# Attention tower: the PSUM banks of the scores apart from those of all other work, v times W0 per tile, and the rounding of q and k on GpSimd

## What is computed

```
h = conv1d(sign(x), sign(kernel), 3 taps), bias and batch norm      # 4 x 748 x 64
z = layernorm(h)
qkv = z @ Wqkv + bqkv; q, k, v = reshape(qkv, (3, b, n, d, h))     # 8 heads of 64
score = einsum('bnqh,btqh->bnth', q, k) * d ** -0.5
attn = softmax(score, axis=1)
av = einsum('bnnh,bnqh->bnqh', attn, v)       # only the DIAGONAL of attn is used
h = h + av.reshape(b, n, d * h) @ W0 + b0
h = h + tree_ffn(layernorm(h))                # 8 levels of a binary tree, a matrix per node
```

## Time and profile before

| | |
|---|---|
| median of 3 runs (lowest to highest) | 580.06 us (578.53 to 587.96) |
| the profiled execution | 581.13 us, of which the span is 579.4 us |
| PE busy | 403.5 us (70%), 2782 matmuls |
| DVE busy | 372.9 us (64%) |
| POOL busy | 307.8 us (53%) |
| ACT busy | 277.9 us (48%) |
| mean granted TensorE clock | 0.849 |

### The profile page before, as it was taken

One profiled execution on the slowest core, in us unless ns is written; L12 is line 12 of the kernel. 1 busy time (PEld: TensorE's weight loads), 2 busy tenths in 40 slices (PEclk: granted clock), 3 DMA queues, 4 the chain that ended last, 5 costly groups with the idle time before them and its releaser, 6 DMA issues.

```text
span 579.4 us, 8416 instructions
## 1 busy us (share of the span) xinstructions
PE 403.5 (70%) x2782; PEld 286.3 (49%) x2782; DVE 372.9 (64%) x605; ACT 277.9 (48%) x615; POOL 307.8 (53%) x354
## 2 busy tenths in 40 slices
PE   1335688887987898888858898622314999287781
PEld 1224566565655565556645665411213777154550
DVE  0756757668677667774678586872982999733431
ACT  1344578768667866776637577410201010044541
POOL 2665308563355177843456771398746677752211
PEclk9977789989889987988869789955555999689997
DMA  4251404319969123212303120084004110200000
GB/s 115 70 120 47 115 13 107 92 42 215 193 127 158 36 67 79 59 37 66 81 0 80 37 72 1 7 124 75 12 12 126 31 41 24 76 9 4 5 6 10
DMA packets 57822, 37.53 MB, mean 65 GB/s; under 512 B 30846, under 2 KB 56429, under 8 KB 57772
## 3 DMA queue, kind: packets, MB, share of 16 engines
q1 hardware_dynamic: 54030, 33.96, 26.7%
q0 software_dynamic: 2944, 2.45, 1.5%
q10 hardware_dynamic: 800, 0.49, 0.3%
HBM read 11.33 MB, written 9.56 MB: 36 GB/s over the span
## 4 chain that ended last, share of the span: by engine, by line
PE 41%; DVE 24%; ACT 16%; issue 8%; POOL 7%; DMA 3%; ACTq 0%; SPq 0%; DVEq 0%; POOLq 0%
PE Z L834 11%; ACT Z L1099 7%; PE Z L963 4%; PE Z L790 4%; DVE lm L1456 4%; PE Z L746 4%; PE Z L737 4%; PE Z L792 3%; DVE nm L1258 3%; DVE va L1449 3%; ACT k L1043 3%; ACT q L1043 2%; PE Z L965 2%; DVE va L1284 2%; PE Z L815 2%
## 5 line engine op out<-in xcount | busy, mean ns | idle before, releaser
L1258 DVE TENSOR_REDUCE nm<-Z 125x1 f32<-125x748 f32 x192 | 172.8, 931 | 94.4 <-PE Z L834 91.8
L1099 ACT ACTIVATE Z<-Z,nm 125x748 f32<-125x748 f32 x192 | 164.9, 860 | 74.8 <-DVE nm L1258 74.6
L834 PE MATMUL Z<-pool_a 128*125 128x512 f16 (+1 forms) x768 | 162.7, 357 | 18.9 <-ACT Z L1099 12.6
L834 PEld LDWEIGHTS Z<-pool_a 128*125 128x125 f16 x768 | 98.6, 151 | 62.3 <-ACT Z L1099 20.9
L667 POOL DMA_INDIRECT out<-lm,va x44 | 43.1, 979 | 59.4 <-DVE lm L1462 52.7
L545 POOL TENSOR_TENSOR pool_a<-q,pool_a 128x748 f16<-128x748 f32 x16 | 26.2, 1635 | 60.4 <-DVE pool_a L1221 60.3
L1456 DVE TENSOR_REDUCE lm<-va 128x64 f32<-128x512 f32 x44 | 45.2, 1027 | 1.3
L790 PE MATMUL Z<-va,xhT 128*125 128x128 f16 x192 | 33.1, 257 | 17.4 <-ACT Z L1099 17.4
L1178 ACT COPY va<-Z 32x512 f32<-32x512 f32 x48 | 27.5, 573 | 34.5 <-PE Z L969 34.5
L1099 ACT ACTIVATION_READ_ACCUMULATOR Z<-Z,nm 125x1 f32 x192 | 39.5, 206 | 0.0
L737 PE MATMUL Z<-xhT,wq 128*128 128x249 f16 (+2 forms) x256 | 33.1, 278 | 8.7 <-ACT Z L1099 7.6
(11 more groups left out here) (208 smaller groups left out, 690.1 us busy)
## 6 DMA issues: line engine op xcount, KB each, us to landing
pool_a<-pool_a SPq DMA_DIRECT2D x64, 187.0 KB, 3.3
pool_a<-pool_a SPq DMA_DIRECT2D x64, 93.5 KB, 2.2
sorted_rows<-zrow SPq DMA_DIRECT2D x1, 3864.0 KB, 22.7
va<-sorted_rows SPq DMA_DIRECT2D x11, 276.0 KB, 5.4
w<-in_L_ffn_w2s SPq DMA_DIRECT2D x1, 2048.0 KB
lm<-in_x SPq DMA_DIRECT2D x4, 375.0 KB
pool_a<-in_L_ffn_w2s SPq DMA_DIRECT2D x1, 1024.0 KB
out<-lm,va POOLq DMA_INDIRECT x44, 2.2
```

What stands on the lines that cost most here:

```text
L834: last = mm(z[0:XP, c0:c1], kst[:, u % 3, a, hd, KST[t]:KST[t] + XP], qst[:, u % 3, hd, c0:c1], start=(a == 0), stop=(a == 1))
L1099: sc_.activation(z, z, ACT.Exp, bias=nm[0:XP, u % 4, i:i + 1], accum_out=sm[0:XP, u % 4, i:i + 1]).then_inc(s_fa, 1)
L1258: v.tensor_reduce(nm[0:XP, u % 4, i:i + 1], zone(("s", u, i))[0:XP, 0:N], X, ALU.max, negate=True).then_inc(s_max, 1)
```

## The change

Scores rotate over the three double zones Z[0] to Z[2] with semaphores of their own (s_score, s_exp). All other jobs alternate between two single banks, the halves E[0] and E[1] of Z[3]. Jobs are cut to fit one bank: a projection in two parts (class 1 and 2; class 0), the diagonal issued in three thirds of four matmuls but one job, transposes, ranks in halves, logits in three. For batches 0 to 2, v times W0 is done per token tile for all eight heads ("yt": three matmuls of 512 columns) and after all four pairs have their weights; for batch 3 per pair in two parts ("yp"). `add_heads` becomes a tree: four chained additions per tile (256, 128, 64 and 64 elements). The rounding of q and k is done by POOL from unit 2 on. POOL's and DVE's work of the tree stage moves to other phases. At the start, SP waits for the first part of x before it sends the second; ACT sends its half of Wqkv after the first copy; DVE makes all low halves of Wqkv and those of q and k of unit 0; the first four projections use the four zones directly; FIRST holds only "xb" 2, "xb" 3 and "cv" 2.

```diff
+PSUM_AT = {1: 0, 2: 249, 0: 512}
+PARTS = {1: (1, 2), 2: (0,)}
...
-        FIRST = [("q", 0), ("k", 0), ("q", 1), ("k", 1), ("xb", 2), ("xb", 3), ("xh", 1), ("cv", 2)]
+        FIRST = [("xb", 2), ("xb", 3), ("cv", 2)]
...
-            if 1 <= u <= NU and i == 0:
-                f.append(("d", u - 1))
-            if u + AHEAD < NU and i in (1, 3):
-                f.append(("qk"[i // 2], u + AHEAD))
...
-            if 3 <= u <= NU and i == 5:
-                f.append(("y", u - 1))
-            if b >= 0 and ph == 2:
-                f += {5: [("t", b)], 8: [("l", b, 0)], 10: [("l", b, 1)]}.get(i, [])
-            if b >= 1 and (ph == 3 if b < B - 1 else ph == 1) and i == 7:
-                f.append(("r", b - 1))
-            if b == B - 1 and ph == 3 and i == 11:
-                f.append(("r", b))
+            if 1 <= u <= NU and i < 3:
+                f.append(("d", u - 1, i))
+            if u + AHEAD < NU and 3 <= i <= 6:
+                f.append(("q" if i < 5 else "k", u + AHEAD, 2 - i % 2))
+            f += {(0, 1): [("xh", 1)], (0, 2): [("wt", 0)], (0, 7): [("wm", 0)], (0, 8): [("xh", 2)], (0, 9): [("cv", 3)],
+                  (0, 11): [("wt", 1)], (1, 7): [("wm", 1)], (1, 8): [("xh", 3)], (1, 9): [("wt", 2)],
+                  (1, 11): [("wm", 2)], (2, 7): [("cb", 0)], (2, 9): [("w1", 0)]}.get((u, i), [])
+            if 0 <= b < B - 1 and ph < 2 and i in (7, 9, 11):
+                f.append(("yt", b, 3 * ph + (i - 7) // 2))
+            if u == NU - 2 and i in (7, 8, 10, 11):
+                f.append(("yp", LASTB + i // 10, (0, 1)[i in (8, 11)]))
+            if NU - 1 <= u <= NU and i in (7, 9):
+                f.append(("yp", u - 1, (i - 7) // 2))
+            if 0 <= b < B - 1 and ph == 3:
+                f += {7: [("t", b, 0)], 8: [("t", b, 1)], 9: [("l", b, 0)], 10: [("l", b, 1)], 11: [("l", b, 2)]}.get(i, [])
+            if 1 <= b and ph == 2 and i in (7, 9):
+                f.append(("r", b - 1, (i - 7) // 2))
...
         def zone(f):
-            return Z[(number[f] + 3) % 4]
+            return E[number[f] % 2]
...
             load_x(0)
+            sp.wait_ge(s_xin[0], 16)
             load_x(1)
...
             rstd1(0)
-            w_lo(0)
             x_lo(0)
-            w_lo(1)
+            rstd1(1)
...
             def part_lo(kind, w):
                 n = "qk".index(kind)
                 c = w % 2
+                if w >= 2:
+                    pool.wait_ge(*evacuated(kind, w))
+                    pool.wait_ge(s_st[(w - 2) % 3], 16 * 8 * ((w - 2) // 3 + 1))
+                    gp.tensor_copy(hl[:, c, n, 0, 0:N], (q32, k32)[n][:, c, 0:N]).then_inc((s_qc, s_kc)[n], 1)
...
+            def add_heads(b, t):
+                k = NT * b + t
+                pool.wait_ge(s_wyv, k + 1)
+                if t == 0:
                     pool.wait_ge(s_hb, b + 1)
+                hv = xrow[0:XP, k, C_H:C_ID]
+                pw = prod[0:XP, k % 2, 0:8 * D]
+                for n in (4 * D, 2 * D, D):
+                    link(gp.tensor_tensor(pw[:, 0:n], pw[:, 0:n], pw[:, n:2 * n], ALU.add))
+                gp.tensor_tensor(hv, hv, pw[:, 0:D], ALU.add).then_inc(s_hy, 1)
...
-                if 0 <= b < B - 1 and ph == 3:
-                    path_masks(b, pool, gp, link)
-                if 1 <= b and ph == 0:
-                    leaf_masks(b - 1, pool, gp, link)
-                if b >= 2 and ph == 0:
-                    own_slots(b - 2)
-                if 0 <= b < B - 1 and ph == 1:
+                if 0 <= b < B - 1 and ph < 2:
+                    for t in range(3 * ph, 3 * ph + 3):
+                        add_heads(b, t)
+                if u == NU - 2:
+                    add_pair(LASTB)
+                if NU - 2 <= u < NU:
+                    add_pair(u - 1)
+                if 0 <= b < B - 1 and ph == 2:
                     ln2_squares(b)
                     ln2_rstd(b)
                     ln2_x(b)
+                if 1 <= b and ph == 0:
+                    path_masks(b - 1, pool, gp, link)
+                if 1 <= b and ph == 1:
+                    leaf_masks(b - 1, pool, gp, link)
+                if b >= 2 and ph == 3:
+                    own_slots(b - 2)
...
-                if number[f] >= 4:
-                    pe.wait_ge(*freed[order[number[f] - 4]])
+                if number[f] >= 2:
+                    pe.wait_ge(*freed[order[number[f] - 2]])
...
             def scores(u, i):
                 hd, t = divmod(i, NT)
-                z = take(("s", u, i))
+                n = 2 * NT * u + i
+                z = Z[n % 3]
+                if n >= 3:
+                    pe.wait_ge(s_exp, n - 2)
+                else:
+                    pe.wait_ge(s_first, n + 2)
...
+            def weigh_heads(b, t):
+
+                k = NT * b + t
+                dve.wait_ge(s_at, NPAIR * (b + 1))
+                dve.wait_ge(*full(("yt", b, t)))
+                if k >= 2:
+                    dve.wait_ge(s_hy, k - 1)
...
-                    if u + AHEAD < NU and i in (3, 5):
-                        hi_cast("qk"[i // 4], u + AHEAD)
...
+                    if 0 <= b < B - 1 and ph == 2 and i == 2:
+                        ln2_sums(b)
+                    if 0 <= b < B - 1 and ph == 3 and i == 0:
+                        ln2_sumsq(b)
```

More of the change, by code:

```diff
@@ L250, in tower, with whole, jobs @@
+            if b == B - 1 and ph == 1:
+                f += {7: [("t", b, 0)], 8: [("t", b, 1)], 9: [("l", b, 0)], 10: [("l", b, 1)], 11: [("l", b, 2)]}.get(i, [])
+            if b == B - 1 and ph == 3 and i in (7, 9):
+                f.append(("r", b, (i - 7) // 2))
+            return f
+        def whole(f):
+            return f if f[0] != "d" else f[:2]
+        def jobs(u, i):
+            return [whole(f) for f in fills(u, i) if f[0] != "d" or f[2] == 2]
         BY_ACT = ("q", "k", "xb", "xh", "wt", "cb", "w1", "t", "l")
@@ L784, in heads_out, with pair_out @@
                 pe.wait_ge(*xhat_ready(GROUPS_FOR["v"][b]))
+                r0, g = v_tile(b, t)
+                for a in range(2):
+                    mm(z[0:XP, :], xhT[:, r0:r0 + XP], mw[:, a, g * H * D:(g + 1) * H * D], start=(a == 0), stop=False)
+                mm(z[0:XP, :], pick[:, g, 0:XP], cb[:], start=False, stop=True).then_inc(s_full, 1)
+            def pair_out(w, n):
+                b, j = divmod(w, NPAIR)
+                z = take(("yp", w, n))
                 js = slice(j * P, (j + 1) * P)
-                for t in range(NT):
+                for t in range(4 * n, min(4 * n + 4, NT)):
                     r0, g = v_tile(b, t)
-                    zt = z[0:XP, t * P:(t + 1) * P]
+                    zt = z[0:XP, t % 4 * P:(t % 4 + 1) * P]
                     for a in range(2):
@@ L800, in w1_T, with x2_T @@
                                     idf[0:NODES - P, 0:NODES - P]).then_inc(s_full, 1)
-            def x2_T(b):
-                z = take(("t", b))
+            def x2_T(b, n):
+                z = take(("t", b, n))
                 pe.wait_ge(s_xh2, b + 1)
-                for t in range(NT):
-                    last = nc.tensor.transpose(z[0:D + 1, t * P:(t + 1) * P], xrow[:, b * NT + t, 0:D + 1], idf[:])
+                for t in range(3):
+                    last = nc.tensor.transpose(z[0:D + 1, t * P:(t + 1) * P], xrow[:, b * NT + 3 * n + t, 0:D + 1], idf[:])
                 last.then_inc(s_full, 1)
@@ L812, in logits, with ranks @@
                     pe.wait_ge(s_b1, 16)
[L813 to L815 removed]
+                    pe.wait_ge(*freed["t", b, 1])
+                for t in range(2):
+                    last = mm(z[:, t * 256:(t + 1) * 256], xT2[:, (2 * n + t) * P:(2 * n + t + 1) * P], w1T[:],
                               start=True, stop=True)
                 last.then_inc(s_full, 1)
[L819 to L820 removed]
+            def ranks(b, n):
+                z = take(("r", b, n))
                 pe.wait_ge(s_m7, b + 1)
[L822 to L824 removed]
+                for t in range(3):
+                    mm(z[:, t * P:(t + 1) * P], tri[:], m7[:, b * NT + 3 * n + t, :], start=True, stop=False)
+                    last = mm(z[:, t * P:(t + 1) * P], ones[:], run[:, 3 * n + t, :], start=False, stop=True)
                 last.then_inc(s_full, 1)
```

320 lines of the change are left out of this document (158 added, 162 removed).

## The result

The changed kernel takes 577.36 us (median of 20 runs, 569.20 to 584.34), the one before 583.49 in the same session (20 runs). The ratio is 0.989, with a 95% interval of 0.985 to 0.993: a gain of 1.1%, where I had forecast 4% (557 against 580.06). The time lies in the range, which began at 536 and ended at 583; less than a third of the gain is there, and by the 2% bound the answer is "no change". The profiled execution of the changed kernel is 569.47 us, at the fast end of its runs, and the one before 581.13. So the two traces show 11.7 us, of which the medians keep 6.

What follows compares the result with a forecast made beforehand. No engine was over 90% busy in units 4 to 15; work alternated through a shared ring of four double banks. From 581.13, terms -15, -9.5, -10, -5, +10.5, 0 gave 552; clock +6 gave 558, 557 as median; range 536 to 583.

Steps and rivals of the forecast that it cites:

- the unit: Score loop, units of batches 0 to 2 with "yt": 15.1 us each, against 18.9 now in units 4 to 7.
- Rival 4: Start: it gives little, as jobs in two small banks or late loads still wait; 572 us, chance 0.13.
- the place of the loss: Units 8 to 15: DVE waits 8 us for POOL's additions, with shorter waits behind; unit 10 becomes 32 us.
- Rival 1: POOL is worse than costed: casts at 2.1 us add 2.2 per unit; 570 us, chance 0.15.
- Rival 2: POOL's waits hardly show: units 8 to 15 lose 2 x 9 less; 538 us, chance 0.14.
- the clock's term: Whole loop: +6 us for time at half clock, on a sum of 552 us that has full clock throughout.
- Rival 3: TensorE at 1.2 GHz for half of units 4 to 15, after DVE's wait idles PE: 600 us, chance 0.10.
- the terms named for units 12 to 15: Like units 8 to 11, plus 3 for "yp", 4 for ln2_sumsq's wait and the ranks of batch 1: 86 against 75.5.
- units 1 to 3: These three units take 18.5 + 15.5 + 15.5 us against 59.1, a term of -9.5.
- The start: Up to unit 1: first maximum at 42, 9.5 earlier, unit 0 then 20 us, first diagonal at 62; -15 us.
- the tail at 0: After the scores: 56 us from path_masks(2) to the last matmul before the overflow slots, as before; change 0.
- the last of the signs: After the scores: the last chain longer than 56 us because own_slots(0) is in its way.

Runs made afterwards that it cites:

- experiment 5: Changed kernel with the old order of the start on POOL and DVE: 582.75 us, ratio 1.003 to the kernel before.
- experiment 2: Changed kernel with path_masks ahead of qk_lo on POOL and the ranks two steps later: 554.17 us, ratio 0.956 to the kernel before.
- experiment 7: Changed kernel with both own_slots at the very end of POOL's loop: 570.41 us, ratio 0.978 to the kernel before.
- Experiment 10: Changed kernel with path_masks ahead of qk_lo, ranks two steps later, wlow cleared by DVE and own_slots(0) moved last: 544.65 us, ratio 0.932 to the kernel before.
- experiment 6: Changed kernel with 45 unread matmuls in step 2 of units 10 and 14: 573.46 us, ratio 0.988 to the kernel before.
- experiment 1: Kernel before with only the changed start (order on POOL and DVE, loads, places of unit 0's jobs): 584.26 us, ratio 1.011 to the kernel before.
- experiment 9: Kernel of Experiment 10 without SP's wait before sending the second part of x: 544.45 us, ratio 0.935 to the kernel before.
- experiment 4: Changed kernel with wlow cleared by DVE instead of POOL: 568.99 us, ratio 0.974 to the kernel before.

## Why the prediction was right in its places and wrong in its size

**Right: the unit.** 15.1 us was forecast; units 4 to 6, 8 and 9 took 15.1 to 15.9. By the waits of DVE in units 4 to 7, its maxima wait for PE for 4.1 us, where it was 21.2 before, and all of the change but the start's order accounts for 12 us of the first four units (experiment 5). Rival 4 (jobs in two small banks still wait) fell as far as the loop goes.

**Right: the place of the loss.** DVE waits for POOL's additions at the start of units 10 and 14, 1.3 us more for tile 5 (1.7 forecast), PE waits 1.7 us for `leaf_masks` in unit 10 (2 forecast) and 0.7 in unit 14, and `ln2_sumsq` waits 4.2 us in unit 15 (4 forecast). The first wait was 5.8, not 8, since POOL was faster than I took it: a cast 0.81 us (1.0 taken), the tree of a tile 2.0 (2.2 taken). Rival 1, a cast near the 2.13 of the compare, is out. Rival 2 (waits that hardly show) is out too: experiment 2 gets 19 to 23 us by moving the block that makes them, and the ranks with it.

**Wrong: the clock's term.** I reckoned every unit at the full clock and laid +6 us over the whole loop for all that the clock does. Units 12 to 15 ran at 0.75 and cost 19.0 us in place of 10.5. Not in unit 14: it took 36.1 us, where I had 35 (32 and the 3 for "yp"), and it takes 36.0 at 0.70 as well (experiment 7). POOL's chain sets its first 19.5 us, and in its last us PE waits for DVE's block of the ranks (for 1.3 us at 0.58, for 3.8 at 0.70). The miss is in unit 15: 26.9 us at 0.69, where my terms left 20.8. The same unit took 24.4 at 0.78 and 30.9 at 0.56. So it is there that the clock is paid, at 6.5 us between these two. Rival 3 had the mechanism, a wait on DVE leaves PE idle and the clock falls, but I asked only whether it would hold for half the loop.

That unit 14 came out so near is luck in part: the first wait was 2.2 us shorter than forecast and the time behind it longer, at a clock of 0.50, where I had reckoned with 1.00. Units 10 and 11 came out near only together: I had 32 and 18.5, they took 24.6 and 24.1, 48.7 in place of 50.5. Experiment 10 says what the waits weigh. It shortens units 12 to 15 by 10.2 us, of which DVE's direct waits for POOL in units 13 to 15 are 8.9 (11.3 in the changed kernel, 2.4 left); the other 1.3 us are the clock, which rose from 0.75 to 0.86 there, and the ranks' later place, not told apart.

That the idle stretch makes the clock fall is not shown in full: the changed kernel has 0.50 from the middle of the gap on, but in experiment 6 the gap was filled and the clock fell after two shorter ones. The Trainium skill ("TensorE: Matmul & The Clock Gate", What's actually happening) states that activity releases the throttle. Units 4 to 7 agree (PE busy 87%, clock 0.97), but units 12 to 15 of the kernel before had 0.86 with PE busy for 90%, so it is no help to size the term.

Three sums in the prediction are wrong by themselves. Twelve score tiles at half clock and the jobs doubled make 26 us, not 23. Columns that took 19.75 us and now take 15 are a third more per time, not a quarter. And the terms named for units 12 to 15 make 88, not 86. The first two sized the clock's term.

**Wrong: units 1 to 3**, forecast -9.5, measured -3.5. It is all in unit 1: 25.2 us, where I had put 18.5 without a working; units 2 and 3 took 15.7 and 14.8 (15.5 each). In unit 1 DVE is in the centering of the last group until 68.5, PE waits 4.6 us, and its next score tiles take 1.2 to 1.5 us in place of 0.8. Nor do the two gains add that I had added: experiment 1 has nothing at unit 4 from the new start alone, experiment 5 has 12 us from the rest alone, and both together have 16.

**The start**, -12.8 in place of -15, was nearer than its terms. The first maximum came 4.6 us earlier than before, not 9.5; unit 0 then took 17.5 us and not 20, which is luck. Two terms were wrong. SP's wait for the first part of x I had put at nothing. In DVE's timeline the second part's signs now begin at 13.53 (before: 11.60) and the centering of group 0 at 18.77 (16.56), 2.2 us later, and without the wait the first maximum is 1.7 us earlier (experiment 9). And two instructions of the centering of group 2 took 2.08 and 2.00 us in place of 0.56, while POOL made the products of q and k (`qk_prod`, 41.9 to 45.7).

**Wrong: the tail at 0.** It is +4.2. `own_slots(0)` stands ahead of `path_masks(2)` (the last of the signs I had named for "wrong"), and experiment 7 takes 4.1 us off by moving it. The other part I had not seen: the clearing of `wlow` on POOL now falls on the slot's instruction of DVE. In the profile it blocks it for 8.17 us; experiment 4 takes 6.4 us off the tail. Before, it had cost 4 us in the same way (4.21). The Trainium skill ("SBUF — State Buffer", Who interferes with whom) states that a VectorE instruction in a two-port mode and GpSimd exclude each other for a whole instruction, and that `tensor_scalar`, which this one is, can enter such a mode. The trace agrees to 0.03 us: the two end at 400.71 and 400.74.

**The profile and the median.** I had carried the profile over to the median by the 1.1 us of the kernel before; for the changed kernel it was 7.9 the other way. Its executions of 569.2 and 569.5 us had a mean clock of 0.83, the longest, 584.3, had 0.80. Units 7 and 8, the same code, took 32.3 us at 1.00 in the changed kernel's profile and 39.1 to 39.3 at 0.78 in those of experiments 4, 5 and 6. So the two units alone can make 7 us between executions. That the changed kernel's other runs lost it there is likely, but they have no trace.

The sum of the misses in the profile is then 2.2 at the start, 6.0 in units 1 to 3, 8.5 in units 12 to 15 and 4.2 in the tail, 20.9, less 3.6 that units 4 to 11 gained more than forecast and less the 6 that I had allowed: 11.3. That is the difference between the 23 us forecast and the 11.7 found. The other 9 us up to 577 are the median's, 7.9 and 1.1.

## What to carry to other kernels

When work is moved to a helper engine, write down its order and ask of each long block which in-order engine waits for what stands behind it; a block of 9 us in the wrong place, with the ranks that depend on it, cost 3% here, and two casts a unit nothing that the total shows. Follow such a chain to its end: behind the first wait of 5.8 us came three more. Price the clock unit by unit, and as a range: the same unit took 24.4 or 30.9 us in different kernels, and the one profiled execution lay 8 us below the median. Look for what covers a wait before filling it: 45 matmuls in a gap won nothing where POOL's chain set the time. Two gains at the same place, here an earlier start and a faster ring, are not to be added; and a long clearing of memory belongs on an engine, and at a time, where no chain runs beside it.

## What the runs showed of the hardware

- A VectorE instruction on 6 elements per partition took 8.17 us beside a GpSimd clearing of 64 x 10368, 0.81 and 0.17 in two kernels in which the clearing ran elsewhere.
- A GpSimd cast of 128 x 748 from fp32 to fp16 took 0.807 us, less than half of the one-operand compare of nearly that size (2.13).

```profile
L558 POOL CAST pool_a<-q 128x748 f16<-128x748 f32 x14 | 11.3, 807 | 43.9 <-ACT q L1083 43.3
```

- The same code ran a unit in 17.24 us at a granted clock of 1.00 and in 21.21 at 0.81, in two executions in which PE had the same work.
- 45 unread matmuls kept the clock at 1.00 across a gap of 6 us and won nothing: the unit took 36.0 us with them and 36.1 without.
- One unit took 24.4, 26.9, 28.8 and 30.9 us at mean clocks of 0.78, 0.69, 0.62 and 0.56 (PE's busy time grew as much), another 36.1 and 36.0 us at 0.58 and 0.70, where other engines set its time.
